# Slot-by-slot messages, an unnormalised router and residual rows behind a square root in a graph-attention and expert layer

## The chip, the cores and the metric

One core of a Trainium2 chip runs the whole kernel in one launch. The metric is device microseconds, from the start of the execution to its end; lower is better.

## The reference, cut to what matters

6250 nodes with 256 features, 106,250 edges sorted by destination (each node has an edge to itself), 8 heads of 32, 8 experts of width 1024, each token to the best two.

```python
e = leaky_relu(a_src[src] + a_dst[dst], 0.2)
e = exp(e - m[dst]);  alpha = e / segment_sum(e, dst)[dst]
out = segment_sum(xh[src] * alpha[:, :, None], dst) + bias
out = (out - mean(out, 0)) * rsqrt(var(out, 0) + eps) * gamma + beta     # over the nodes
x = x + (out + layernorm(x))
logits = layernorm(x) @ Wr + br                                       # 8 experts
top_p, top_idx = top_k(softmax(logits), 2);  weights = top_p / top_p.sum()
x = x + sum over the two of  weights * expert(layernorm(x))               # gelu between two products
```

## The kernel before, in words

Nodes lie in 49 tiles of 128 rows, edges in 879 slots of 128; a slot belongs to one tile of destinations. All five engines run their own streams and meet at semaphores that are written out by hand. There are five stages.

**Stage 1** makes the node table in HBM. **The edge stage** goes over 110 batches of 8 slots (`EB`; the last has 7). GpSimd issues one indirect gather for each slot (line 1072) into a ring of four batches (`gather_ring`); it may go on to batch b when TensorE has summed batch b-4. VectorE runs `score(b)` (four operations of 64 elements, lines 1103 to 1112), its part of preparing the experts' weights (`vector_w1`, `vector_w2`), `sum_picks(b+1)` (line 1095), `message(b)` (line 1117: all 8 slots' rows, 2048 elements, times the heads' weights, which ScalarE's exponential has put into PSUM) and then `adds(b-1)`: for each slot of the batch before, the sum that TensorE made is added to its tile of `acc` (line 1090; the tile's number comes from a register that `load_tiles` fills on VectorE's queue, line 1054). Each addition waits for the one before it. TensorE runs `picks(b+2)` (lines 932 and 1172), `keep_clock` (line 1161: 16 products whose result nobody reads), then one product for each slot (line 1196, two instructions of 264 columns) into four banks (`AGG`), so slot s waits for the addition of slot s-4. When the last slot of a group of 7 tiles is in, `divide` (lines 1127 and 1130) normalises the group; all seven groups become final within the last batches, and before the last batch three of them are divided in one go.

**The norm stage**: TensorE turns `acc` in 13 chunks of 4 tiles (line 1415) through three pairs of banks, VectorE measures each (line 1357), ScalarE puts it back turned (`keep`, line 1428) and, after each chunk, makes two rows of the residual (`scalar_resid`, line 1341). Behind the last chunk stand two more residual rows and then the root of the variance (line 1438). VectorE folds scale and shift from the root, and **stage 3** begins: TensorE makes the normalised rows tile by tile through six banks, VectorE adds the residual (`x1`, line 1481, which waits for its residual row) and measures the row (line 1486), ScalarE copies the router's 8 columns out of the bank (`keep_logits`, line 1719), which frees it, and makes a later residual row.

**Routing** (`vector_route`): a chain of dependent VectorE operations of 392 elements (49 tiles by 8 experts). The logits are scaled and biased, the largest taken off, exponentials made on ScalarE, summed, inverted and multiplied; then the two largest are found and the lists of tokens for each expert built (lines 1644 to 1664, `token_idx`). Meanwhile ScalarE normalises `acc` in 49 rows (`rows`, line 1736) and then issues two transfers of the tokens' weights (`meta`, lines 1752 and 1754). **The expert stage**: GpSimd gathers token rows (line 2013) once `token_idx` and `meta` are in HBM, TensorE turns them (`turn`, line 1932), ScalarE and VectorE split them into two float16 parts, and TensorE computes 56 slots of two products (lines 1951 and 1968).

## Time and profile before

| what | us |
|---|---|
| median of 3 runs (1958.91 to 1962.71) | 1960.81 |
| the profiled execution's own time | 1963.34 |
| its span, from first to last instruction | 1961.5 |
| first gather of the edge stage | 93.9 |
| last addition of the edge stage starts | 1228.00 |
| first tile of stage 3 (line 1481) | 1264.59 |
| first product of the experts (line 1951) | 1368.78 |
| busy: TensorE / VectorE / ScalarE / GpSimd | 1738.8 / 1434.2 / 1118.5 / 1211.7 |

The stages follow each other, so the busy shares over the whole span (89, 73, 57 and 62%) do not say what bounds a stage: TensorE's share contains the products that only keep it busy, and GpSimd's is made in one stage. What a change is worth has to be read where it is made.

### The profile page before, as it was taken

The numbers are of one execution on the slowest core, as the hardware profiler recorded it, in microseconds if no ns is written. First come the engines' busy times: TensorE is split into PE (matmuls) and PEld (weight loads), VectorE is DVE, ScalarE is ACT, GpSimd is POOL, SyncE is SP. The second block draws the span as 40 slices with busy tenths as digits, with TensorE's granted clock in tenths as the row PEclk, the third lists the DMA queues.
The fourth block names the chain that finished last, engine by engine and source line by source line (L and its number), as shares of the span: only waits on it lengthen the run. The fifth ranks groups of instructions, "written<-read, shape, count | busy, mean of one in ns | idle before, by whom it ended". The sixth has DMA issues, their size and how long they took to land.

```text
span 1961.5 us, 36447 instructions
## 1 busy us (share of the span) xinstructions
PE 1738.8 (89%) x10852; PEld 1204.0 (61%) x10852; DVE 1434.2 (73%) x3115; ACT 1118.5 (57%) x2444; POOL 1211.7 (62%) x1150
## 2 busy tenths in 40 slices
PE   7759899899999999999999987645999999999997
PEld 5535554454555555555454544533889898989896
DVE  7787777878778787887777878798666666666664
ACT  5666666767667576676667762661443434343443
POOL 1277777777777777777777774101466565656553
PEclk9979999999999899999999999875999999999999
DMA  5554546455464554555556452387233333333322
GB/s 171 163 147 121 146 141 164 120 154 157 141 165 135 138 157 141 167 143 135 151 140 167 121 138 57 127 297 197 32 49 51 50 50 50 50 51 50 50 42 34
DMA packets 142680, 233.52 MB, mean 119 GB/s; under 512 B 31127, under 2 KB 107553, under 8 KB 141313
## 3 DMA queue, kind: packets, MB, share of 16 engines
q0 software_dynamic: 62800, 147.54, 31.9%
q1 hardware_dynamic: 69765, 81.13, 13.2%
q10 hardware_dynamic: 9932, 2.52, 0.8%
q8 instruction: 101, 1.65, 0.4%
q14 instruction: 82, 0.67, 0.1%
HBM read 188.81 MB, written 43.15 MB: 118 GB/s over the span
## 4 chain that ended last, share of the span: by engine, by line
PE 64%; DVE 15%; issue 8%; DMA 5%; POOL 5%; ACT 2%; DVEq 1%; ACTq 0%; SPq 0%; POOLq 0%
PE bank L1196 15%; PE bank L1951 14%; PE bank L1968 14%; PE bank L1161 12%; POOL gather_ring L1072 5%; PE bank L1172 3%; DVE acc L1090 3%; DMA gather_ring<-node_table,src_slot 2%; DVE gather_ring L1117 2%; PE bank L932 2%; DMA w_stage<-in_L_ffn_W 2%; PE bank L678 1%; PE bank L1932 1%; DVE acc L629 1%; ACT acc L1428 1%
## 5 line engine op out<-in xcount | busy, mean ns | idle before, releaser
L1072 POOL DMA_INDIRECT gather_ring<-node_table,src_slot x879 | 837.5, 953 | 268.2 <-issue 251.7
L1196 PE MATMUL bank<-gather_ring,onehot 128*128 128x264 f32 x1758 | 491.6, 412 | 75.4 <-DVE acc L1090 73.2
L1090 DVE TENSOR_TENSOR acc<-acc,bank 128x264 f32 x879 | 376.9, 429 | 195.1 <-PE bank L1196 123.7
L1196 PEld LDWEIGHTS bank<-gather_ring,onehot 128*128 128x128 f32 x1758 | 303.8, 190 | 252.8 <-DVE acc L1090 208.1
L1161 PE MATMUL bank<-ones 128*128 128x512 bf16 x1760 | 414.3, 390 | 0.0
L2035 POOL DMA_INDIRECT out_rows<-y,token_idx x105 | 202.3, 1926 | 219.8 <-DMA out_rows<-y,token_idx 150.1
L2003 ACT ACTIVATE hid<-bank,cols 128x256 f32<-128x256 f32 (+1 forms) x448 | 210.3, 551 | 141.4 <-PE bank L1951 138.0
L1161 PEld LDWEIGHTS bank<-ones 128*128 128x128 bf16 x1760 | 168.4, 100 | 194.9 <-issue 22.2
L1951 PE MATMUL bank<-xe,w_hi 128*128 128x256 f16 (+1 forms) x1792 | 284.5, 267 | 0.7 <-ACT hid L2003 0.5
L1968 PE MATMUL bank<-w,hid_hi 128*128 x1680 | 278.3, 273 | 0.1
L1217 ACT ACTIVATE onehot<-iota_free,neg_dst 128x128 f32<-128x128 f32 x880 | 267.3, 386 | 0.0
L1117 DVE TENSOR_TENSOR gather_ring<-gather_ring,bank 128x2048 f32<-128x2048 f32 x110 | 250.4, 2276 | 2.0 <-ACT bank L1234 2.0
L2013 POOL DMA_INDIRECT xs<-x_rows,token_idx x105 | 141.9, 1352 | 152.8 <-DVE token_idx L1664 120.8
L1951 PE MATMUL bank<-xe,w_lo 128*128 128x256 f16 (+1 forms) x896 | 236.1, 267 | 0.0
L1234 ACT ACTIVATE bank<-zbuf 128x64 f32<-128x64 f32 x110 | 25.0, 228 | 363.4 <-DVE zbuf L1112 363.4
L1968 PE MATMUL bank<-w,hid_lo 128*128 x840 | 229.0, 273 | 0.0
L1882 DVE TENSOR_SCALAR hid_hi<-hid,cols 128x1024 f16<-128x1024 f32 (+1 forms) x112 | 90.0, 804 | 150.1 <-ACT hid L2003 150.0
L1951 PEld LDWEIGHTS bank<-xe,w_hi 128*128 x1792 | 168.9, 98 | 22.1 <-issue 1.6
L1968 PEld LDWEIGHTS bank<-w,hid_hi 128*128 128x128 f16 x1680 | 164.3, 98 | 20.2 <-issue 0.8
L1989 ACT ACTIVATE xe<-bank 128x512 f16<-128x512 f32 (+1 forms) x56 | 32.0, 571 | 226.4 <-PE bank L1932 226.4
L1172 PE MATMUL bank<-pick_parts,onehotT 128*128 x880 | 114.9, 195 | 44.4 <-DVE gather_ring L1117 15.6
L1172 PEld LDWEIGHTS bank<-pick_parts,onehotT 128*128 128x128 bf16 x880 | 81.6, 98 | 109.4 <-issue 85.8
(288 smaller groups left out, 2049.2 us busy)
## 6 DMA issues: line engine op xcount, KB each, us to landing
w_stage<-in_L_ffn_W SPq DMA_DIRECT2D x16, 1024.0 KB, 7.3
dst_row<-dst_rows SPq DMA_DIRECT2D x110, 128.0 KB, 3.3
gather_ring<-node_table,src_slot POOLq DMA_INDIRECT x879
w_split<-w_out SPq DMA_DIRECT2D x32, 256.0 KB, 2.9
w<-w_split SPq DMA_DIRECT2D x8, 1024.0 KB, 11.9
node_table<-acc SPq DMA_DIRECT2D x24, 264.0 KB
xt<-in_x SPq DMA_DIRECT2D x24, 256.0 KB, 3.0
r_ring<-in_x SPq DMA_DIRECT2D x6, 896.0 KB, 10.6
```

The costliest lines, as they stand in the source:

```text
L1072: e.indirect_dma_start(out=gather_ring[:, b % GB, j, :], out_offset=None, in_=node_table, in_offset=bass.IndirectOffsetOnAxis(ap=src_slot[ ...
L1090: e.tensor_tensor(a, a, bank[AGG[s % len(AGG)]][:, 0:ROW].rearrange("p (a c) -> p a c", a=1), ALU.add).then_inc(added, 1)
L1117: e.tensor_tensor(rows, rows, weights(b).rearrange("p j (h a) -> p j h a", a=1) .broadcast_to([P, EB, HEADS, DH]), ALU.mult).then_inc(mess ...
L1161: e.matmul(idle_bank[:, :].rearrange("p (k n) -> p k n", k=2), halves[:, 0:P], halves.rearrange("p (a n) -> p a n", a=1).broadcast_to([P, ...
L1172: made = e.matmul(bank[PICKS[b % 2]][:, j * 3 * PICK:(j + 1) * 3 * PICK], onehotT[:, b % 2, j * P:(j + 1) * P], pick_parts[:, bass.ds(tile ...
L1196: e.matmul(bank[AGG[s % len(AGG)]][:, 0:ROW], onehot[:, b % OHB, j, :], gather_ring[:, b % GB, j, :], start=True, stop=True).then_inc(summ ...
L1217: made = e.activation(onehot[:, b % OHB, j, :], iota_free[:, :], ACT.Abs, bias=neg_dst[:, s:s + 1])
L1951: made = e.matmul(to, m[:, k, expert, at:at + P].rearrange("p a m -> p (a m)"), xe[:, q, x_, 0:w], start=(k == 0 and n == 0), stop=(k == K ...
L1968: made = e.matmul(bank[YB[q]][:, i * D:(i + 1) * D], a[:, q, c, ts], w2[:, expert, b, c, :].rearrange("p a d -> p (a d)"), start=(c == 0 a ...
L2003: made = e.activation(hid[:, i % HR, c, 0:w], bank[HB[2 * h + c // 2]][:, c % 2 * PW:c % 2 * PW + w], ACT.Gelu, bias=col_of(s, B1_COL + h ...
L2013: e.indirect_dma_start(out=xs[:, t % XR, :], out_offset=None, in_=x_rows, in_offset=bass.IndirectOffsetOnAxis(ap=token_idx[:, t:t + 1], ax ...
L2035: e.indirect_dma_start(out=out, out_offset=bass.IndirectOffsetOnAxis(ap=token_idx[:, t:t + 1], axis=0), in_=y[:, s % 2, t - first_tile(s), ...
```

## The change

In the edge stage the message of a batch is made slot by slot, and behind the message of slot s comes the addition of slot s-3; `sum_picks` and `load_tiles` stand ahead of them, and TensorE waits for each slot's message by itself, runs `picks(b+2)` behind the products of batch b, and spreads its 16 idle products as 8 ahead of the batch and one ahead of each slot. In the norm stage no residual row stands between the chunks: all 24 come behind the root, and a root of a constant is taken ahead of the chunks. In routing the probabilities are never normalised: the two largest of the biased logits are taken, and the weights come from one exponential of their difference (49 elements); two operations on the logits move ahead, between the steps of the last variances, and ScalarE makes two groups of rows before its exponential. At the start of the expert stage `vector_columns` stands behind the first `split_input`, and TensorE's first `turn` ahead of its wait for the experts' numbers.

```diff
-            def message(b):
-                rows = gather_ring[:, b % GB, :, 0:D].rearrange("p j (h d) -> p j h d", d=DH)
-                e.wait_ge(weighed, 2 * b + 1)
-                e.tensor_tensor(rows, rows, weights(b).rearrange("p j (h a) -> p j h a", a=1)
-                                .broadcast_to([P, EB, HEADS, DH]), ALU.mult).then_inc(messages, 1)
+            def message(b, j):
+                row = gather_ring[:, b % GB, j, 0:D].rearrange("p (h d) -> p h d", d=DH)
+                if j == 0:
+                    e.wait_ge(weighed, 2 * b + 1)
+                e.tensor_tensor(row, row, weights(b)[:, j, :].rearrange("p (h a) -> p h a", a=1)
+                                .broadcast_to([P, HEADS, DH]), ALU.mult).then_inc(messages, 1)
+
+            def messages_and_adds(b):
+                for j, s in enumerate(slots_in(b)):
+                    message(b, j)
+                    if s >= ADDS_BEHIND:
+                        add(*divmod(s - ADDS_BEHIND, EB))
...
-            for b in range(LAST_B):
+            for b in range(BATCHES):
+                load_tiles(e, b)
                 score(b)
                 vector_w1(e, b)
                 vector_w2(e, b)
-                sum_picks(b + 1)
-                message(b)
-                if b:
-                    divide_final((b - 1) * EB)
-                    adds(b - 1)
-            adds(LAST_B - 1)
-            score(LAST_B)
-            message(LAST_B)
-            divide_final(LAST_B * EB)
-            adds(LAST_B)
+                if b + 1 < BATCHES:
+                    sum_picks(b + 1)
+                messages_and_adds(b)
+                divide_final(slots_in(b)[-1] + 1 - ADDS_BEHIND)
+            for s in range(USED - ADDS_BEHIND, USED):
+                add(*divmod(s, EB))
             divide_final(USED)
...
             for b in range(BATCHES):
-                if b + 2 < BATCHES:
-                    picks(b + 2)
...
-                keep_clock(e)
+                keep_clock(e, IDLE_PRODUCTS // 2)
                 e.wait_ge(onehot_made, b + 1)
                 e.wait_ge(weighed, 2 * b + 2)
-                e.wait_ge(messages, b + 1)
                 for j, s in enumerate(slots_in(b)):
+                    keep_clock(e, IDLE_PRODUCTS // 2 // EB)
+                    e.wait_ge(messages, s + 1)
...
+                if b + 2 < BATCHES:
+                    picks(b + 2)
...
+            e.activation(sd_col, ones[:, 0:KD], ACT.Sqrt)
             for c in range(CHUNKS):
                 keep(c)
-                for n in range(2 * (c - 2), 2 * (c - 1)):
-                    if 0 <= n:
-                        scalar_resid(e, n)
             e.wait_ge(var_known, 1)
             e.activation(sd_col, var_col, ACT.Sqrt, bias=eps[:, :]).then_inc(sd_made, 1)
-            for n in range(2 * (CHUNKS - 2), RESID_AHEAD):
+            for n in range(RESID_AHEAD):
                 scalar_resid(e, n)
...
             variances(1)
+            pr = prob[:, :, :]
+            e.wait_ge(logits_kept, NT)
+            vector_order.of(e.tensor_tensor(pr, pr, logits[:, :, :], ALU.add))
             second(1)
+            e.wait_ge(vector_order.sem, vector_order.n)
+            vector_order.of(e.tensor_tensor(pr, pr, rs1[:, :].rearrange("p (n a) -> p n a", a=1).broadcast_to([P, NT, NE]),
+                                            ALU.mult))
             gains(1)
...
-            tt(pr, pr, logits[:, :, :], ALU.add)
-            tt(pr, pr, per_tile(rs1[:, :]), ALU.mult)
             tt(pr, pr, per_expert(br_row[:, :]), ALU.add)
-            reduce_e(peak, pr, ALU.max)
-            e.tensor_tensor(pr, pr, per_tile(peak), ALU.subtract).then_inc(logits_shifted, 1)
-            e.wait_ge(exps_made, 1)
-            reduce_e(peak, pr, ALU.add)
-            chain(e, e.reciprocal(peak, peak))
-            tt(pr, pr, per_tile(peak), ALU.mult)
             for c, best in enumerate((w0, w1)):
                 F3 = first[:, c, :, :]
                 reduce_e(best, pr, ALU.max)
+                if c:
+                    e.tensor_tensor(peak, w1, w0, ALU.subtract).then_inc(logits_shifted, 1)
...
-            tt(peak, w0, w1, ALU.add)
-            chain(e, e.reciprocal(peak, peak))
-            vector_order.of(e.tensor_tensor(meta[:, :, 0:1].rearrange("p n a -> p (n a)"), w0, peak, ALU.mult))
-            e.tensor_tensor(meta[:, :, 1:2].rearrange("p n a -> p (n a)"), w1, peak, ALU.mult).then_inc(meta_made, 1)
+            e.wait_ge(exps_made, 1)
+            chain(e, e.tensor_single_scalar(w0, peak, 1.0, ALU.add))
+            chain(e, e.reciprocal(w1, w0))
...
+            for g in range(2):
+                rows(g)
             e.wait_ge(logits_shifted, 1)
-            e.activation(prob[:, :, :], prob[:, :, :], ACT.Exp).then_inc(exps_made, 1)
-            for g in range(GROUPS):
+            e.activation(top[:, 0, :], top[:, 0, :], ACT.Exp).then_inc(exps_made, 1)
+            for g in range(2, GROUPS):
                 rows(g)
...
+            split_input(0)
+            vector_columns(e)
+            e.wait_ge(vector_order.sem, vector_order.n)
             for s in range(2):
                 columns(s)
-            split_input(0)
```

## Rows read from the trace of the kernel before

**Rows 1.** The waits of GpSimd: who waited for whom, us in total, times, longest.
```profile
POOL gather_ring L1072 <- issue: 251.7, 830, 0.3
POOL gather_ring L1072 <- PE bank L1196: 13.4, 48, 0.3
```

**Rows 2.** The gathers by their line: nanoseconds min/median/max, first and last start.
```profile
L1072 POOL DMA_INDIRECT gather_ring<-node_table,src_slot x879: 942/947/2692, 93.9 to 1200.3; - x176
```

**Rows 3.** Timeline of one batch: start us, duration us, instruction, idle before.
```profile
612.19 3.61 PE L1161 MATMUL bank<-ones 128*128 128x512 bf16 x16
...
612.77 0.22 DVE L1103 TENSOR_TENSOR zbuf<-gather_ring,picked 128x64 f32<-128x64 f32 x1
...
614.75 2.28 DVE L1117 TENSOR_TENSOR gather_ring<-gather_ring,bank 128x2048 f32<-128x2048 f32 x1
...
616.94 0.42 DVE L1090 TENSOR_TENSOR acc<-acc,bank 128x264 f32 x1
...
617.58 0.43 DVE L1090 TENSOR_TENSOR acc<-acc,bank 128x264 f32 x1 [0.21 <-DVE acc L1090]
```

**Rows 4.** Timeline of the last batches of the edge stage.
```profile
1148.88 0.94 POOL L1072 DMA_INDIRECT gather_ring<-node_table,src_slot  x1 [0.30 <-issue]
...
1151.73 0.22 DVE L1103 TENSOR_TENSOR zbuf<-gather_ring,picked 128x64 f32<-128x64 f32 x1 [0.97 <-DMA gather_ring<-node_table,src_slot]
...
1200.34 1.81 POOL L1072 DMA_INDIRECT gather_ring<-node_table,src_slot  x1 [0.30 <-issue]
...
1213.25 0.22 DVE L1103 TENSOR_TENSOR zbuf<-gather_ring,picked 128x64 f32<-128x64 f32 x1
...
1228.00 0.43 DVE L1090 TENSOR_TENSOR acc<-acc,bank 128x264 f32 x1 [0.21 <-DVE acc L1090]
```

**Rows 5.** Timeline of the norm stage.
```profile
1230.94 3.68 DVE L1357 BATCH_NORM_STATS2 feat<-bank 128x6 f32<-128x512 f32 x6
...
1232.55 3.05 ACT L1428 ACTIVATE acc<-bank 128x512 f32<-128x512 f32 x6 [17.88 <-DVE feat L1357]
...
1244.18 1.16 ACT L1428 ACTIVATE acc<-bank 128x512 f32<-128x512 f32 x2
...
1244.63 1.29 DVE L1357 BATCH_NORM_STATS2 feat<-bank 128x6 f32<-128x512 f32 x2 [0.66 <-PE bank L1415]
...
1250.31 0.48 DVE L1364 BATCH_NORM_AGGREGATE agg<-feat 128x2 f32<-128x72 f32 x1
...
1255.43 1.28 ACT L1438 ACT_TABLE_LOAD   x1
...
1257.06 0.17 DVE L1385 RECIPROCAL bn_cols<-bn_cols 128x2 f32<-128x2 f32 x1 [3.11 <-ACT bn_cols L1438]
```

**Rows 6.** Timeline, first tile of stage 3.
```profile
1264.59 0.42 DVE L1481 TENSOR_TENSOR acc<-bank,r_ring 128x256 f32<-128x256 f32 x1 [1.89 <-PE bank L1696]
```

**Rows 7.** Timeline of the last variances and the routing.
```profile
1301.36 0.29 DVE L1510 RECIPROCAL rs<-sd 128x21 f32<-128x21 f32 x1 [0.38 <-ACT sd L1728]
...
1304.30 0.57 DVE L1548 TENSOR_TENSOR prob<-prob,br_row 128x392 f32<-128x392 f32 x1
...
1306.53 18.77 ACT L1736 ACTIVATE acc<-acc,shift,gain 128x256 f32<-128x256 f32 x38
...
1308.36 0.56 DVE L1551 TENSOR_REDUCE top<-prob 128x49 f32<-128x392 f32 x1
```

**Rows 8.** Timeline from the tokens' weights to the experts' first products.
```profile
1325.25 27.83 ACTq L1754 DMA_DIRECT2D x_rows<-meta  x1
...
1358.32 1.19 POOL L2013 DMA_INDIRECT xs<-x_rows,token_idx  x1 [120.78 <-DVE token_idx L1664]
...
1367.53 1.09 PE L1932 MATMUL bank<-ident,xs 128*128 128x128 f32 x4 [3.67 <-DMA xs<-x_rows,token_idx]
```

**Rows 9.** Stretches: length, busy us (x instructions) of PE, PEld, DVE, ACT, POOL, clock, DMA share, GB/s.
```profile
1356.30:1358.30 2.00, 0.00 (x0) 0.00 (x0) 1.90 (x5) 0.00 (x0) 0.00 (x0) 0.50 0.00 0
...
1368.70:1371.70 3.00, 2.92 (x14) 2.09 (x15) 0.69 (x1) 0.55 (x1) 1.89 (x2) 0.50 0.32 89
```

More of the change, by code:

```diff
@@ L829, in build_gnn_moe @@
         scalar_order = Order(sem("scalar_order"))
-        AGG = (0, 1, 3, 4)
+        AGG, ADDS_BEHIND = (0, 1, 3, 4), 3
         PICKS = (2, 7)
@@ L1112, in score @@
                 e.tensor_tensor(zbuf[:, 1, :, :], zbuf[:, 1, :, :], zbuf[:, 0, :, :], ALU.subtract).then_inc(scored, 1)
-            def message(b):
-                rows = gather_ring[:, b % GB, :, 0:D].rearrange("p j (h d) -> p j h d", d=DH)
-                e.wait_ge(weighed, 2 * b + 1)
-                e.tensor_tensor(rows, rows, weights(b).rearrange("p j (h a) -> p j h a", a=1)
-                                .broadcast_to([P, EB, HEADS, DH]), ALU.mult).then_inc(messages, 1)
-            def adds(b):
-                load_tiles(e, b)
-                for j in range(len(slots_in(b))):
-                    add(b, j)
+            def message(b, j):
[9 more added lines that the diff above has]
+                        add(*divmod(s - ADDS_BEHIND, EB))
             def divide(g):
@@ L1138, in vector_edges @@
             divided = [0]
-            LAST_B = BATCHES - 1
             e.wait_ge(acc_started, GROUPS)
             sum_picks(0)
-            for b in range(LAST_B):
+            for b in range(BATCHES):
+                load_tiles(e, b)
                 score(b)
@@ L1145, in vector_edges, with keep_clock @@
                 vector_w2(e, b)
-                sum_picks(b + 1)
-                message(b)
-                if b:
-                    divide_final((b - 1) * EB)
-                    adds(b - 1)
-            adds(LAST_B - 1)
-            score(LAST_B)
-            message(LAST_B)
-            divide_final(LAST_B * EB)
-            adds(LAST_B)
+                if b + 1 < BATCHES:
[4 more added lines that the diff above has]
+                add(*divmod(s, EB))
             divide_final(USED)
-        def keep_clock(e):
+        def keep_clock(e, products):
             halves = ones[:, :].bitcast(BF16)
-            for _ in range(IDLE_PRODUCTS):
+            for _ in range(products):
                 e.matmul(idle_bank[:, :].rearrange("p (k n) -> p k n", k=2), halves[:, 0:P],
@@ L1168, in picks @@
                 if b >= 2:
-                    e.wait_ge(messages, b - 1)
+                    e.wait_ge(messages, (b - 1) * EB)
                 tensor_w1_bias(e, b)
@@ L1232, in scalar_edges @@
                 if b >= 2:
-                    e.wait_ge(messages, b - 1)
+                    e.wait_ge(messages, (b - 1) * EB)
                 e.activation(weights(b), zbuf[:, 1, :, :], ACT.Exp).then_inc(weighed, 1)
@@ L1407, in tensor_norm @@
                 if c == 0:
-                    e.wait_ge(messages, BATCHES)
+                    e.wait_ge(messages, USED)
                 if c == 1:
@@ L1578, in vector_route @@
                 if c == 0:
-                    chain(e, e.scalar_tensor_tensor(pr, F3, -2.0, pr, ALU.mult, ALU.add))
+                    chain(e, e.scalar_tensor_tensor(pr, F3, FAR_BELOW, pr, ALU.mult, ALU.add))
             tt(chosen[:, :, :], first[:, 0, :, :], first[:, 1, :, :], ALU.add)
             e.tensor_tensor(chosen[:, :, :], chosen[:, :, :], per_tile(valid[:, :]), ALU.mult).then_inc(chosen_made, 1)
-            tt(peak, w0, w1, ALU.add)
-            chain(e, e.reciprocal(peak, peak))
-            vector_order.of(e.tensor_tensor(meta[:, :, 0:1].rearrange("p n a -> p (n a)"), w0, peak, ALU.mult))
-            e.tensor_tensor(meta[:, :, 1:2].rearrange("p n a -> p (n a)"), w1, peak, ALU.mult).then_inc(meta_made, 1)
+            e.wait_ge(exps_made, 1)
+            chain(e, e.tensor_single_scalar(w0, peak, 1.0, ALU.add))
+            chain(e, e.reciprocal(w1, w0))
+            vector_order.of(e.tensor_copy(meta[:, :, 0:1].rearrange("p n a -> p (n a)"), w1))
+            e.tensor_tensor(meta[:, :, 1:2].rearrange("p n a -> p (n a)"), peak, w1, ALU.mult).then_inc(meta_made, 1)
             def by_expert(psum):
@@ L1683, in vector_route @@
             e.tensor_copy(expert_of_slot[:, :], expert_of_slot_f[:, :]).then_inc(experts_known, 1)
-            vector_columns(e)
         def tensor_stage3(e):
@@ L1738, in rows @@
                 made.then_inc(rows_made, 1)
-            assert GROUPS == RB + 2 and RESID_AHEAD + LATE_AT > RB * NG > 2 * (CHUNKS - 2)
+            assert GROUPS == RB + 2 and RESID_AHEAD + LATE_AT > RB * NG
             for g in range(5):
@@ L1971, in output @@
                 made.then_inc(y_done, 1)
+            for i in range(2):
+                e.wait_ge(rows_stored[i], (STORED[0], ROWS_STORED)[i])
+            turn(0)
             e.wait_ge(experts_known, 1)
-            turn(0)
             for s in range(FS + 1):
```

1 line of the change is left out of this document (removed).

## The prediction

> **What bounds the kernel now.** I read the page's busy shares first, then the chain that ended last, and left both: they mix stages. What decides is read stage by stage in the timeline. In the edge stage the waits of GpSimd come first [rows 1]: 830 of 879 gathers follow the one before after the same 0.3 us, the other 48 were released by TensorE within that same 0.3, so GpSimd was never held up by the ring. With a median gather of 0.947 [rows 2] the pace is 1.25 us a slot, 10.0 a batch, and the whole stretch is 93.9 to 1200.3. VectorE comes second: one batch is 1.98 ahead of the message, 2.19 for it and 8 x 0.64 for the additions, 9.3 in all, since each addition waits 0.21 for its predecessor [rows 3]. So the edge stage can gain only behind the last gather. There VectorE is late: the last batch's score starts at 1213.25 although its gathers were issued at 1200.34, and a batch can be scored 2.85 after its last gather starts (1148.88 to 1151.73, where VectorE did wait for it) [rows 4]. The norm stage is paced by ScalarE: per chunk VectorE measures 1.29 and idles 0.66, and ScalarE spends 1.16 on putting back and the rest on two residual rows; then VectorE waits 3.11 for the root, ahead of which stand two more rows and a table load of 1.28 [rows 5]. Routing is a chain on VectorE alone. From the experts' first product on TensorE sets the time, and nothing there changes.
>
> **Edge loop.** A message of one slot is 256 elements; the addition of 264 takes 0.43, so I take 0.42. Independent VectorE instructions overlap by 0.09 (614.75 + 2.28 against 616.94) [rows 3]. A pair of message and addition is then 0.67, and the 0.21 that an addition waits for its predecessor lies under the message between them; I take 0.70. A batch is 1.98 + 5.6 and some 0.25 for the register load, which no longer lies under a long message: 7.8. That is 1.5 less work than before and 2.2 under the gathers' 10.0, so VectorE waits for gathers instead, and the 106 us that are freed over 110 batches buy nothing. TensorE has the same instructions as before, and with them it never held a gather up [rows 1]. Its reordering costs nothing under the same 10.0. Bounds for the pair: 0.64 below (an addition and its wait) and 0.42 + 0.64 = 1.06 above (nothing overlaps).
>
> **End of the edge stage.** Divisions read and write only `acc`; beside one of them the last gather took 1.81 instead of 0.95 [rows 4]. The new order has one division more among the gathers, which costs the gathers 0.9 (0 to 2.6). Batch 108's last gather, 7 paces before 1200.34, starts at 1191.6; with 0.9 and 2.85 its score starts at 1195.3. Then 1.5 up to the messages, 5.6, and one division. A division: from 1213.25 to 1228.00 before lie 1.3 of score, 2.2 of message, three divisions and 6 x 0.64, so 2.5 each, 2.7 with the wait. VectorE is free at 1205.1; gathers are there at 1204.1 (up to 1206). I take 1205.4. The last batch: 1.3, 7 x 0.70 = 4.9, a division 2.7, and 1.3 up to the start of the last addition: 1215.6 against 1228.00. **Gain 12.4** (10 to 13.5). The two other divisions that stood here now lie ahead, beside waiting time.
>
> **Chunks.** Count from the last addition's start, L. Before, the measuring started at L+2.9 and ended at L+22.3 [rows 5]. After, three chunks still take 3.7 (to L+6.6), but the fourth needs a bank that ScalarE has put back. ScalarE began this at L+4.55, behind its transfers; the new root of a constant puts 1.28 + 0.3 ahead of it, then 1.1 to put back and about 1.2 for TensorE: L+8.2. From there VectorE needs 1.25 a chunk, and TensorE and ScalarE need less: nine chunks and 0.5 for the single tile end at L+20.0; I add 0.5 for transposes at half clock, as the stage starts after an idle TensorE. **Gain 1.8** (0.4 to 3.4).
>
> A table load is 1.28 here, and the reciprocal that waits for the root behind it starts 0.35 after it [rows 5]. The Trainium skill (ScalarE: Activation LUTs, What ACT_TABLE_LOAD costs) adds a drain of about 1.38 us to each switch. No drain shows in these rows; by the page the constant's root would cost the chunks 1.4 more, and the sum would be 1.4 smaller.
>
> **Root.** After: the variance is known 1.8 behind the chunks, ScalarE has the table and no row ahead, so the root is done at 2.2, and VectorE comes to its wait at 3.6 (1250.31 to 1257.06 less 3.11). **Gain 3.1** (2.5 to 3.1).
>
> **Stage 3.** What is late next are the 24 residual rows, at 18.77 / 38 = 0.494 each for rows of this form [rows 7]: 11.9, so from 2.2 to 14.1 behind the chunks, and ScalarE's first copy of router columns, which frees a bank, stands behind them. VectorE starts tile 0 at 3.6 + 7.5 (1257.06 to 1264.59 [rows 5, 6]) = 11.1. Six banks last to tile 6, at 0.66 to 0.7 a tile at 15.1 to 15.3; its product is ready about 1.0 after the first copy, 15.1. ScalarE then catches up (copy and row 0.55 against 0.66). **Cost 0** (to 1.9 if a row takes 0.59).
>
> **Routing.** Between the end of the bias addition (1304.30 + 0.60) and the first maximum (1308.36) stand a maximum, a subtraction, the exponential, a sum, a reciprocal and a product, all gone: 3.46. Two additions and products of 0.60 ahead move to where VectorE waits 0.38 for each root [rows 7]; they spill about 0.15: 1.05. A subtraction of 49 elements comes in: 0.13. The small exponential comes after two groups of rows (14 x 0.494 = 6.9) and a table load, about 0.8 before the choice ends, and what waits for it lies under the count's product on TensorE. **Gain 4.4** (3.8 to 4.6).
>
> **Experts' start.** Gathers need `token_idx` and the landed `meta`. The second meta transfer is issued at 1325.25 and holds its queue 27.8; nothing moves after 1356.3, and the gather starts at 1358.32 [rows 8, 9]. It is issued when the rows are done, and these move only 2.4 ahead of stage 3's end, not 4.4: the cover of 2.0 shrinks to about nothing. Cost 0.3 (0 to 2). Neither moved order gains much: `turn(1)` waits for its rows until 1367.53 [rows 8] in either order, and the first product stands behind it. Gain 0.1. TensorE ran at half clock for the first 3.0 us of the stage [rows 9]; when the clock rises is not tied to the stage, so 1 more or 1.7 less is open both ways.
>
> **Sum.** 12.4 + 1.8 + 3.1 + 0 + 4.4 - 0.3 + 0.1 = 21.5. The span 1961.5 goes to 1940.0 and its execution's 1963.34 to 1941.8; the runs' median, 2.5 below that execution, 1960.81 to 1939.3.
>
> **Rivals.** (a) *Gains eaten by what is late next*: rows at 0.59 stall the six banks by 1.9, meta binds and takes 2.0 of the routing, the last gathers land 2 later, the half clock stays 1 longer. For it: three covers shrink to under 0.5 each. Against: each was worked out as just enough. Gain 14.6 to 17: about 1945. (b) *VectorE becomes the edge stage's bound*: the other side. If the additions keep their own 0.64 and messages 0.42 apart from them (1.06 a pair), a batch is 2.2 + 8.5 = 10.7 against 10.0, 0.7 x 110 = 77 slower less 21: about 2016. It decides from a pair of 1.0 on. For it: `load_tiles` and each addition's register step stand on the same queue. Against: the wait was 0.21 and the message is longer. The Trainium skill (VectorE: DVE Perf Modes, Side-by-side: where the cycles go) gives each instruction some 150 cycles of start, so cutting a message in eight would add about 1.1 us a batch; the rows' overlap takes most of it back, and either way 10.0 is not reached without the lost overlap. (c) *The batch loop also speeds up*, since messages no longer hold VectorE: it would take 1.5 x 110 off, about 1775. Rows 1 exclude it unless the 0.3 hides a wait. (d) *The end isn't shortened*: the last batch is scored late as before, because TensorE's idle products inside the slots delay additions; then only 9.1 remain: 1951.
>
> **How the numbers follow.** Forecast 0.70, (a) 0.18, (b) 0.04, (c) 0.01, (d) 0.07. The forecast's terms have ends 10 + 0.4 + 2.5 - 1.9 + 3.8 - 2 = 12.8 and 13.5 + 3.4 + 3.1 + 4.6 + 0.1 = 24.7, and the clock 1.7; all ends together are unlikely. 1934.5 to 1947 holds the forecast and (a). 0.2% (about 4 us) is what this kernel's measurement can tell from none. Faster 0.95, same 0.01, slower 0.04.
>
> **What would show it.** Message and addition starting about 0.7 apart; gathers still 0.947; GpSimd's first wait at the end of the stage; VectorE waiting for gathers in most batches; the last addition near 1216; no wait of 3 us for the root; tile 6 without a stall; the first maximum right behind the bias addition; the expert gather released by `token_idx` or by a transfer. Gathers above 0.97 us or a pair above 0.95 would make the forecast wrong.

## The result, and the profile after

The changed kernel takes 1942.72 us (median of 4 runs, 1942.01 to 1945.27) against 1960.68 (4 runs, 1958.91 to 1962.71) for the kernel before on the same chip: ratio 0.9908, 95% interval 0.9894 to 0.9922, so 18 us faster. A second set on another chip gave 1946.71 against 1962.67, ratio 0.9918 (0.9904 to 0.9931). The forecast was 1939.3 with a range from 1934.5 to 1947.0.

The profiled execution has a span of 1940.7 (1942.65 with what lies around it), 20.8 under the 1961.5 of before.

**Edge stage.** First the timeline of VectorE inside a batch (line 1118 is a message, line 1090 an addition), then the waits of GpSimd and VectorE for each other's work (us in total, times, longest), with VectorE's waits for gathers in the kernel before at the end:

```profile
610.46 0.41 DVE L1118 TENSOR_TENSOR gather_ring<-gather_ring,bank 128x256 f32<-128x256 f32 x1
610.79 0.42 DVE L1090 TENSOR_TENSOR acc<-acc,bank 128x264 f32 x1
611.13 0.41 DVE L1118 TENSOR_TENSOR gather_ring<-gather_ring,bank 128x256 f32<-128x256 f32 x1
611.46 0.42 DVE L1090 TENSOR_TENSOR acc<-acc,bank 128x264 f32 x1
```

```profile
DVE zbuf L1103 <- DMA gather_ring<-node_table,src_slot: 198.4, 95, 7.3
...
POOL gather_ring L1072 <- issue: 252.8, 837, 0.3
POOL gather_ring L1072 <- PE bank L1193: 12.2, 41, 0.3
```

```profile
DVE zbuf L1103 <- DMA gather_ring<-node_table,src_slot: 25.0, 20, 3.0
```

A message and an addition together take 0.67 from start to start (610.46 to 611.13). GpSimd waits as it did [rows 1], and VectorE now waits 198.4 us for gathers, where it waited 25.0 before.

The end of the stage, where [rows 4] had the last gather at 1200.34, the last score at 1213.25 and the last addition at 1228.00:

```profile
1201.19 0.95 POOL L1072 DMA_INDIRECT gather_ring<-node_table,src_slot  x1 [0.30 <-issue]
...
1202.93 2.02 DVE L1132 TENSOR_TENSOR acc<-acc 128x1792 f32<-128x1792 f32 x1
1204.87 0.22 DVE L1103 TENSOR_TENSOR zbuf<-gather_ring,picked 128x64 f32<-128x64 f32 x1
...
1214.60 0.43 DVE L1090 TENSOR_TENSOR acc<-acc,bank 128x264 f32 x1 [0.21 <-DVE acc L1090]
```

**Norm stage and stage 3.** The rows that answer to [rows 5, 6]: the table load and the root of a constant ahead of the chunks, the aggregate behind the last chunk, the root, the 24 residual rows behind it, the operation of VectorE that needs the root, the first and the third `x1`.

```profile
1218.56 1.28 ACT L1431 ACT_TABLE_LOAD   x1 [12.26 <-issue]
1219.86 0.20 ACT L1431 ACTIVATE bn_cols<-ones 128x2 f32<-128x2 f32 x1
...
1234.57 0.48 DVE L1363 BATCH_NORM_AGGREGATE agg<-feat 128x2 f32<-128x72 f32 x1
...
1236.37 0.29 ACT L1435 ACTIVATE bn_cols<-bn_cols,eps 128x2 f32<-128x2 f32 x1 [1.22 <-DVE bn_cols L1372]
...
1236.57 11.89 ACT L1340 ACTIVATE r_ring<-r_ring,x_shift,rstd 128x256 f32<-128x256 f32 x24
...
1238.11 0.16 DVE L1384 RECIPROCAL bn_cols<-bn_cols 128x2 f32<-128x2 f32 x1
...
1245.28 0.42 DVE L1478 TENSOR_TENSOR acc<-bank,r_ring 128x256 f32<-128x256 f32 x1 [1.54 <-PE bank L1692]
...
1247.54 0.42 DVE L1478 TENSOR_TENSOR acc<-bank,r_ring 128x256 f32<-128x256 f32 x1 [0.37 <-ACT r_ring L1340]
```

The table load now stands ahead of the chunks and the 3.11 wait for the root is gone. The third `x1` did not wait for a residual row, though its line names one: the third of the 24 rows was ready near 1238.1 (1236.57 and three times 0.495). The product that it adds ended at 1247.43, at half clock.

**Routing and the experts' start.** The rows that answer to [rows 7, 8]:

```profile
1284.53 0.56 DVE L1551 TENSOR_TENSOR prob<-prob,br_row 128x392 f32<-128x392 f32 x1
1285.13 0.56 DVE L1554 TENSOR_REDUCE top<-prob 128x49 f32<-128x392 f32 x1
...
1304.04 30.48 ACTq L1752 DMA_DIRECT2D x_rows<-meta  x1
...
1334.22 0.27 DVE L1661 SCALAR_TENSOR_TENSOR token_idx<-upto 128x105 int32<-128x105 f32 x1
...
1339.93 1.19 POOL L2015 DMA_INDIRECT xs<-x_rows,token_idx  x1 [115.79 <-DMA x_rows<-meta]
...
1348.00 0.63 PE L1951 MATMUL bank<-xe,w_hi 128*128 128x256 f16 x2
```

The first maximum follows the bias addition at once. But the first expert gather is no longer released by the token list: the list is ready at 1334.5, the gather starts at 1339.93, released by the transfer of the `meta` columns. Part 4 of the page, the chain that ended last, has the same as one step:

```profile
1304.04 35.00 DMA x_rows<-meta
```

**Where the 20.8 us are**, as differences of the two timelines. Before, the token list's instruction started at 1357.33.

| from, to | before | after | gain |
|---|---|---|---|
| start to first gather | 93.94 | 92.95 | 1.0 |
| first gather to last addition | 1134.06 | 1121.65 | 12.4 |
| last addition to first `x1` | 36.59 | 30.68 | 5.9 |
| first `x1` to last `x1` | 34.36 | 35.10 | -0.7 |
| last `x1` to token list | 58.38 | 53.84 | 4.5 |
| token list to first expert gather | 0.99 | 5.71 | -4.7 |
| expert gather to first expert product | 10.46 | 8.07 | 2.4 |
| first expert product to the end | 592.7 | 592.7 | 0.0 |

### The profile page after: what moved, and what is told of

Its sections match the earlier page's. It is cut to its first block and busy times, and to the rows that moved or that the text cites. A ratio compares the mean times of both kernels' runs of the same rounds, so it can differ in the third digit from the quotient of the medians.

```text
span 1940.7 us, 37977 instructions
## 1 busy us (share of the span) xinstructions
PE 1692.2 (87%) x10851; PEld 1186.6 (61%) x10851; DVE 1420.1 (73%) x3880; ACT 1118.9 (58%) x2445; POOL 1214.0 (63%) x1150
## 3 DMA queue, kind: packets, MB, share of 16 engines
q1 hardware_dynamic: 69765, 81.13, 13.4%
## 5 line engine op out<-in xcount | busy, mean ns | idle before, releaser
L1159 PE MATMUL bank<-ones 128*128 128x512 bf16 x1759 | 553.4, 393 | 76.9 <-ACT gather_ring L1234 65.9
L1193 PE MATMUL bank<-gather_ring,onehot 128*128 128x264 f32 x1758 | 566.7, 405 | 51.0 <-DVE gather_ring L1118 50.6
L1193 PEld LDWEIGHTS bank<-gather_ring,onehot 128*128 128x128 f32 x1758 | 294.8, 195 | 261.4 <-DVE gather_ring L1118 219.3
L1090 DVE TENSOR_TENSOR acc<-acc,bank 128x264 f32 x879 | 367.9, 419 | 18.7 <-PE bank L1193 17.5
L1118 DVE TENSOR_TENSOR gather_ring<-gather_ring,bank 128x256 f32<-128x256 f32 x879 | 359.5, 409 | 0.3 <-ACT bank L1233 0.3
L1103 DVE TENSOR_TENSOR zbuf<-gather_ring,picked 128x64 f32<-128x64 f32 x110 | 24.8, 226 | 202.2 <-DMA gather_ring<-node_table,src_slot 198.4
L1883 DVE SCALAR_TENSOR_TENSOR hid_lo<-hid,cols,hid_hi 128x1024 f16<-128x1024 f32 (+1 forms) x112 | 136.4, 1217 | 4.0
## 6 DMA issues: line engine op xcount, KB each, us to landing
w<-w_split SPq DMA_DIRECT2D x8, 1024.0 KB, 13.8
```

The source lines that it names most:

```text
L1090: e.tensor_tensor(a, a, bank[AGG[s % len(AGG)]][:, 0:ROW].rearrange("p (a c) -> p a c", a=1), ALU.add).then_inc(added, 1)
L1118: e.tensor_tensor(row, row, weights(b)[:, j, :].rearrange("p (h a) -> p h a", a=1) .broadcast_to([P, HEADS, DH]), ALU.mult).then_inc(messa ...
L1159: e.matmul(idle_bank[:, :].rearrange("p (k n) -> p k n", k=2), halves[:, 0:P], halves.rearrange("p (a n) -> p a n", a=1).broadcast_to([P, ...
L1193: e.matmul(bank[AGG[s % len(AGG)]][:, 0:ROW], onehot[:, b % OHB, j, :], gather_ring[:, b % GB, j, :], start=True, stop=True).then_inc(summ ...
L1883: e.scalar_tensor_tensor(hid_lo[:, q, cs, 0:w], hid[:, i % HR, :, 0:w], col_of(s, HS_COL), hid_hi[:, q, cs, 0:w], ALU.mult, ALU.subtract). ...
```

## The experiments

### One part of the change at a time

`x_edges`, `x_norm` and `x_route` are the kernel before with the edge loop, the norm stage, or the routing of the change alone (the last with the order of the first turns).

> The kernel before with the edge loop of the change alone. Theory: the batches' pace stays the gathers', so only the end of the stage moves: last addition 13.4 us earlier, as in the whole change (its trace: 1228.00 to 1214.60), and the time comes out 13 us under the kernel before (near 1947.5). Rival: the edge loop is worth less alone, because the norm stage behind it then still waits for its chunks; under 11 us. If the loop's pace had changed as well, over 30 us.

> The kernel before with the norm stage of the change alone (constant root ahead, residual rows behind the variance's root). Theory: the trace of the whole change has 5.9 us less between the last addition and the first x1, and 0.7 us more between there and the end of the halves' variances, so 5.2 us earlier: near 1955.5. Rival, as predicted: 4.9 with no loss behind it. Rival on the other side: the residual rows, late now, cost stage 3 what the root gave; no change.

> The kernel before with the routing of the change alone, and the order of the first turns with it. Prediction's own step: 4.4 us less (near 1956.3). Theory now: the token list is ready 4.5 us earlier, but the first expert gather then waits for the meta columns, whose last packets land only behind the last four loads of W2; those do not end earlier by as much, so the gather gains under 1 us and the time 0 to 3 us (some 2 us come from the bias load that is then no longer beside the second pair of gathers).

| run | median us | before, same chip | ratio, 95% interval |
|---|---|---|---|
| x_edges | 1951.79 | 1961.91 | 0.9943 (0.993 to 0.9956) |
| x_norm | 1958.29 | 1961.91 | 0.9975 (0.9967 to 0.9984) |
| x_route | 1961.15 | 1961.91 | 0.9997 (0.9988 to 1.0006) |

They save 10.1, 3.6 and 0.8, together 14.5 of the 16 to 18 that the whole change saves. Each is less than its part of the table above. The traces show a loss of the right kind, but the profiled executions of `x_edges` and `x_norm` (1954.95 and 1960.70) lie 3.2 and 2.4 above their medians, so the losses read from them are larger than the medians' share.

*Edges.* From the first gather to the last addition it takes 1121.8, as in the changed kernel, so the gain of this stretch is there (the 13.4 of the expectation held 1.0 of an earlier start). The time fell by less than the 11 of the rival, but not for its reason: from the last addition to the first `x1` it took 35.9, and 36.6 before, so the norm stage did not wait for more. Behind it stage 3 took longer: 38.25 from first to last `x1` in place of 34.36.

*Norm.* Likewise: from the last addition to the first `x1` 31.5 instead of 36.6, then 38.05 for stage 3. Both losses are of one kind: the granted clock of TensorE is half for 6.8 us from tile 30 on, where five `x1` come 1.13 apart instead of 0.66 (2.6 and 2.7 us), and more of the first tiles run at half clock than before (1.2 us in `x_edges`, 0.9 in `x_norm`).

*Routing.* The theory held. The token list is 4.5 earlier against the last `x1` than before; the gather is not (60.5 behind the last `x1`, 59.4 before):

```profile
1350.80 0.27 DVE L1664 SCALAR_TENSOR_TENSOR token_idx<-upto 128x105 int32<-128x105 f32 x1
...
1357.46 1.19 POOL L2018 DMA_INDIRECT xs<-x_rows,token_idx  x1 [122.20 <-DMA x_rows<-meta]
```

By itself the routing part is not to be told from no change.

### What the meta columns wait for

`a_w2_held` is the changed kernel with one wait on SyncE's queue:

```diff
+            e.wait_ge(meta_stored, 16 * 2)
             for ee in range(EARLY_W2, NE):
                 load_w2(ee)
```

> The changed kernel, with the last four loads of W2 held until the meta columns have landed. Theory: the meta columns trickle behind those 4 MB (a few dozen of their packets in 2 us while the loads run), so alone they land near 1320 instead of 1339.0; the first expert gather starts at 1335.2 with the token list, 4.7 us earlier; of this 2 us may go again to the bias load beside the second pair of gathers: 2 to 5 us faster than the changed kernel (1938 to 1941). Rival: the meta columns are slow by themselves, 6,250 packets of 16 bytes; then they land no earlier, the loads end later, and the time is the same or up to 10 us longer.

It took 1942.6 against 1961.91, ratio 0.989 (0.9876 to 0.9905). That is 0.002 to 0.003 better than the changed kernel, with overlapping intervals: the wait is shown by the trace, a gain in time is not.

```profile
1331.18 2.04 SPq L1783 DMA_DIRECT2D w<-w_split  x4
1337.18 0.27 DVE L1661 SCALAR_TENSOR_TENSOR token_idx<-upto 128x105 int32<-128x105 f32 x1
1337.75 1.50 POOL L2016 DMA_INDIRECT xs<-x_rows,token_idx  x1 [113.20 <-DVE token_idx L1661]
...
1341.79 0.35 ACTq L1754 DMA_DIRECT2D b_all<-in_L_ffn_b  x1
```

The gather is released by the token list again, 0.57 behind it. Both theories were half right. In the changed kernel the last tenth of the 6,250 packets of 16 bytes lies between 1321.5 and 1337.7, beside the loads of W2, and ends when these end; without them it ends at 1329.5 with the first packet at 1310.7, so the meta columns also need 19 us of their own beside the rows' stores, and 1320 was wrong. The loads, now late, run beside the gathers, as does the 1 MB bias load: from the token list to the first product are 11.8, against 13.8. So 5.1 are won at the gather and 3.1 of them given back behind it.

The other traces agree. In the eleven profiles where these loads are not held, the last small packet ends 0.5 to 1.0 us behind the last packet of the loads, though the transfer was issued 7.1 to 9.4 us ahead of these four loads. Measured from the last `x1`, it ends at 57.3 in the kernel before and at 57.3 in the changed one, while the token list went from 58.4 to 53.8.

The Trainium skill (DMA: Bandwidth & Descriptors, Queues, rings and completion order) says that each DMA engine takes turns between the queues that have work for it, a packet at a time. The two queues do advance together here; that the small packets all but stop beside the large ones (14 or 15 of them in each 2 us from 1328 to 1336) is what the records show, and the page's turns do not explain by themselves.

`a_meta_early` also sends the large transfer sooner and the bias load later:

```diff
             for g in range(2, GROUPS):
                 rows(g)
-            e.wait_ge(meta_made, 1)
-            e.dma_start(x_rows[0:(NT - 1) * P, D:XROW]..., meta[:, 0:NT - 1, :]).then_inc(meta_stored, 16)
+                if g == 2:
+                    e.wait_ge(meta_made, 1)
+                    e.dma_start(x_rows[0:(NT - 1) * P, D:XROW]..., meta[:, 0:NT - 1, :]).then_inc(meta_stored, 16)
...
                     copy_input(s + 1)
+                if s == 0:
+                    e.wait_ge(experts_known, 1)
+                    e.dma_start(b2_all...).then_inc(b2_loaded, 16)
```

> The changed kernel, with the large transfer of the meta columns issued behind the third group of rows (7 rows of ScalarE behind the Exp) and no longer behind the seventh, the last four loads of W2 held until both meta transfers have landed, and the bias load (1 MB) behind the second turn. Theory: the transfer starts near 1295 and not near 1304, has its 6,250 small packets through by 1320, and the loads of W2 are over before the first gathers of expert rows; the token list then releases the first gather (0.6 us behind it), and the first expert product follows 9 us behind the list, as against 13.8 in the changed kernel and 11.8 with the loads held alone: 4 to 5 us faster. Rival: the small packets only share the same DMA engines with the stores of the rows, so the stores end later by what the meta columns take, and the first gather waits for them: same time.

It took 1939.04, against 1946.71 for the changed kernel beside it on the same chip (0.9876, interval 0.9861 to 0.9892, against 0.9918, interval 0.9904 to 0.9931): 7.7 faster, and the intervals do not meet.

> The changed kernel itself, once more, beside the others on one chip, as their yardstick: 18 us under the kernel before, as in its first runs.

```profile
1328.71 2.11 SPq L1780 DMA_DIRECT2D w<-w_split  x4
1336.11 0.27 DVE L1661 SCALAR_TENSOR_TENSOR token_idx<-upto 128x105 int32<-128x105 f32 x1
1336.68 1.50 POOL L2018 DMA_INDIRECT xs<-x_rows,token_idx  x1 [113.24 <-DVE token_idx L1661]
...
1345.01 0.60 PE L1949 MATMUL bank<-xe,w_hi 128*128 128x256 f16 x2
```

The small packets were through later than expected, at 1327.9, still ahead of the list. From the token list to the first product are now 8.9. In the trace of `after_again` they are 13.3 (1337.02 to 1350.32), so 4.4 are explained here, and the two spans differ by 5.3 (1942.7 to 1937.4). The rest of the 7.7 in the medians is not told apart from the spread between executions. Against `a_w2_held` (11.8 from list to first product) two things changed at once, the earlier transfer with its earlier loads and the later bias load; no run tells how the 2.9 divide between them.

### What holds a gather

`a_div_split` is the changed kernel with the product of a division cut by tile:

```diff
-                e.tensor_tensor(rows, rows, acc[:, tiles(g), D:ROW]..., ALU.mult).then_inc(normalised, 1)
+                for n in range(NG):
+                    made = e.tensor_tensor(rows[:, n:n + 1], rows[:, n:n + 1], acc[:, tiles(g), D:ROW]...[:, n:n + 1]..., ALU.mult)
+                made.then_inc(normalised, 1)
```

> The changed kernel, with each division's product of 128x1792 (2.02 us) given out tile by tile, seven products of some 0.33 us. Theory: a GpSimd gather that meets the long product is held until it ends; four are held by 5.4 us together in the changed kernel, three by 3.5 us in the one before. Short products hold none for longer than 0.4 us, as the messages of 0.41 us show: the last gather starts 4 to 5 us earlier (near 1196.5), the time falls by 4 us; each division is 0.3 us longer, the last one on the path. Rival: what holds a gather is the sum of such products' time, not the length of one; then nothing moves, or 0.3 us is lost.

It took 1941.56, 5.2 under the changed kernel beside it (0.9888, interval 0.9871 to 0.9904, which touches that of the changed kernel, 0.9904 to 0.9931). The timeline around one division, first in the changed kernel, then here:

```profile
1190.53 2.02 DVE L1132 TENSOR_TENSOR acc<-acc 128x1792 f32<-128x1792 f32 x1
1190.72 2.67 POOL L1072 DMA_INDIRECT gather_ring<-node_table,src_slot  x1 [0.30 <-issue]
1193.68 0.95 POOL L1072 DMA_INDIRECT gather_ring<-node_table,src_slot  x1 [0.30 <-issue]
```

```profile
1189.84 2.44 DVE L1133 TENSOR_TENSOR acc<-acc 128x256 f32<-128x256 f32 x7
1190.27 1.15 POOL L1072 DMA_INDIRECT gather_ring<-node_table,src_slot  x1 [0.30 <-issue]
1191.72 1.03 POOL L1072 DMA_INDIRECT gather_ring<-node_table,src_slot  x1 [0.30 <-issue]
```

The gather lasts 1.15 instead of 2.67. Over all divisions, four gathers are held by 5.3 us together in `after_again` and six by 1.0 here, and the last gather starts at 1196.81 instead of 1201.05. Not all of that reaches the end: VectorE reaches the last score 1.3 later behind the last gather (a division's products take 2.44 instead of 2.02), and from the first gather to the last addition it takes 1119.2 instead of 1122.2. So the traces show 3.0 of the 5.2; the spans of the two profiles differ by 3.4.

One part of the expectation's argument was poor: a message takes its weights from a PSUM bank and so does not show what a short product of two SBUF operands does; the run does. What the messages do show is that length alone holds no gather. In the kernel before a message took 2.28, more than a division's product, and the gathers beside them took their usual 0.95:

```profile
614.75 2.28 DVE L1117 TENSOR_TENSOR gather_ring<-gather_ring,bank 128x2048 f32<-128x2048 f32 x1
614.92 0.95 POOL L1072 DMA_INDIRECT gather_ring<-node_table,src_slot  x1 [0.30 <-issue]
616.17 0.95 POOL L1072 DMA_INDIRECT gather_ring<-node_table,src_slot  x1 [0.30 <-issue]
```

Of the 270 gathers that met such a message none took over 0.98. The Trainium skill (VectorE: DVE Perf Modes, Two Vector instructions with no wait between them) says that a VectorE instruction with two SBUF tensors reads the second through an interface that GpSimd shares. That fits: the division's product has two SBUF tensors, and the messages and additions, with one operand in PSUM, hold no gather. No run moves an operand of the same product between SBUF and PSUM, so the operand's place as the cause is argued.

### VectorE's room in a batch

`a_load4` and `a_load8` put idle work behind the messages of the odd slots, or of all:

```diff
                     message(b, j)
+                    if j in (1, 3, 5, 7):       # a_load8: range(EB)
+                        vector_order.of(e.tensor_reduce(spare[:, b % 2, j:j + 1], ones..., AX.XY, ALU.add))
```

> The changed kernel, with four more operations in each batch on VectorE (a sum over 128x256 into a spare column, some 0.35 us each, 1.4 us a batch), behind the messages of the odd slots. Theory: the batches' pace is GpSimd's (10.0 us for 8 gathers, VectorE waits 198 us for them, 1.8 a batch), so the last gather starts where it did (1201.2, to 1 us) and the time moves by less than 3 us. Rival, VectorE close to the bound: 1.4 us a batch appear in full or in part, 30 us or more.

> The changed kernel, with eight more operations in each batch on VectorE (one behind every message; each 128x256 summed into a spare column). With four of them the time did not move. Theory: VectorE's slack in a batch is 1.8 us (198 us of waits for gathers over 109 batches); with eight of them at 0.35 us, 2.8 us, the batch is VectorE's, 10.0 + 1.0 us, and the stage 110 us longer, 2055. Rival: their length lies beside waits that VectorE has anyway inside a batch (for products and exponentials), then less than 30 us.

`a_load4` took 1947.05 in one run (1946.71 for the changed kernel): nothing. `a_load8` took 2034.25. The waits of VectorE for gathers in `a_load4`, and the added operations of `a_load8` by their line:

```profile
DVE zbuf L1104 <- DMA gather_ring<-node_table,src_slot: 56.5, 37, 4.2
```

```profile
L1126 DVE TENSOR_REDUCE spare<-ones 128x1 f32<-128x256 f32 x879 | 360.0, 410 | 0.0
```

Each added operation moves the next one's start by 0.333 (0.41 less the overlap). Four a batch are 439 x 0.333 = 146 us: they came out of the 198.4 us of waits, of which 56.5 are left, and the end did not move. Eight are 879 x 0.333 = 293 us; less 198 that leaves 94, and the last addition came 91.7 later (1306.26). The expectation of 110 had taken 0.35 for an operation. So in this kernel, with the work spread evenly over the batches, the wait of the bottleneck's neighbour is a budget that can be read from the profile to a few per cent.

### The distance of the additions, and the idle products

> The changed kernel, with each addition one slot behind its message instead of three. Theory: an addition then waits for the product of the slot before, which waited for its message: a slot's pair is no longer 0.67 us but the chain of semaphore, product (0.61 us) and addition, near 1.0 us; the batch is 2.6 us longer on VectorE, over its slack of 1.8 us, and the stage longer by up to 0.8 us a batch: 1950 to 2035. Rival: the product of 0.61 us fits behind one pair of 0.67 us; then no change to 1 us.

With `ADDS_BEHIND = 1` the time is 1963.97 in one run, all of the gain gone. In its waits the additions now stand for their products, and the pair takes longer every second slot:

```profile
DVE acc L1090 <- PE bank L1193: 150.9, 434, 3.2
```

```profile
628.68 0.42 DVE L1090 TENSOR_TENSOR acc<-acc,bank 128x264 f32 x1
629.02 0.41 DVE L1118 TENSOR_TENSOR gather_ring<-gather_ring,bank 128x256 f32<-128x256 f32 x1
629.67 0.43 DVE L1090 TENSOR_TENSOR acc<-acc,bank 128x264 f32 x1 [0.24 <-PE bank L1193]
```

Two slots take 1.67 instead of 1.34. The last gather starts 5.6 later (1206.81), and the last addition 28.1 behind it instead of 13.4: 20.3 in all. The same budget accounts for this too: no wait of VectorE for a gather is left. Its waits for products, ahead of the scores and for the picks are 150.9, 36.6 and 26.3 (17.5, 3.7 and 10.1 in the changed kernel), 182 more, and the overlap of 0.09 lost at 434 additions is another 39: 221, or 23 over the 198 that there were.

> The changed kernel, with all sixteen idle products of a batch ahead of its slots and none between them. Theory: the pace of 0.67 us a slot is VectorE's (a message of 0.33 us from start to start, an addition the same), the idle product (0.21 us) between two slot products lies beside it; last addition within 0.5 us of the last gather's distance in the changed kernel (13.4 us), time the same. Rival, as predicted with 0.07: the idle products delay the additions, then the distance gets shorter without them between, or longer because all sixteen stand ahead of the last batch's first slot product (1.9 us more).

It took 1942.37 in one run, and the last addition is 13.43 behind the last gather, as in the changed kernel (13.41). In this run the idle products between slots cost nothing, and neither do sixteen ahead.

### Both improvements together

> The changed kernel with both of what helped it: each division's product given out tile by tile, and the meta columns early, the last four loads of W2 held and the bias load late. Theory: the two act in different stages and add up, 4 to 5 us at the gathers' end and 5 to 7 us at the first expert product: near 1935, a ratio of 0.985 to the kernel before. Rival: the norm stage or the loads of W2 take one of them back; then no better than the better of the two alone (0.9876).

It took 1937.55 against 1962.6, ratio 0.9873 (0.9857 to 0.989), the fastest of all kernels here, 7 to 9 us under the changed kernel by the ratios. But it is not told apart from `a_meta_early` (0.9876). The trace has the first expert product 3.9 earlier than `a_meta_early` (1341.14 to 1345.01) and the end only 2.1 earlier; the experts' stage took 594.1 instead of 592.4. Why it took longer stays open.

## Why the prediction was right, and where it was off, point by point

The mechanism was right in the main: nothing in the batch loop, 12 us behind the last gather, the rest in the stages behind. One term, the meta transfer, was mis-sized by 4.4. The time was forecast 3.4 too low.

- **Edge loop.** Forecast 0.70 a pair and no gain from the loop; measured 0.67, and `a_load4` shows that VectorE's time is worth nothing there. Eight messages at 0.33 are 2.7 a batch where the one message took 2.19, so cutting it cost 0.5, and not the 1.1 that the prediction had from the 150 cycles. The "106 us that are freed" are a slip: 1.5 a batch is 165 over 110 batches, and VectorE's waits for gathers grew by 173.
- **End of the edge stage.** Forecast 12.4, with the last addition at 1215.6; measured 12.4 from the first gather on (1214.60, with a start 1.0 earlier). The last score was forecast for 1205.4 and came at 1204.87. The cost of one division more among the gathers was put at 0.9. It was 1.9: four gathers are held in the changed kernel by 5.3 us together, against three by 3.5 before. That the 12.4 still came out is luck in part, for the last batch was 0.5 shorter than forecast (9.7 from its score to the last addition, not 10.2) and the rest lay in a score put 0.3 later than VectorE was free. Over all profiles the stretch from the first gather to the last addition is 1133.0 to 1134.1 in three with the old loop and 1121.6 to 1122.4 in five with the new one, so 11.6 is the better figure.
- **Chunks and root.** Forecast 1.8 and 3.1; measured 2.3 (the aggregate is 19.97 behind the last addition, 22.31 before) and 3.6 (from there to the first `x1` 10.71, 14.28 before). No drain shows at the table load that was moved: ScalarE's next operation starts at 1219.86, 0.02 behind it. The fourth chunk started 8.55 behind the last addition; the forecast said 8.2, though its own terms add up to 8.4. The 0.5 that it added for half clock did not come.
- **Stage 3.** Forecast 0; measured 0.7 in this trace. No stall at tile 6. The 0.7 is TensorE's clock: three products ran at half clock where two did before. In most of the profiles it costs more (below).
- **Routing.** Forecast 4.4; the token list is 4.5 earlier.
- **Meta transfer: the step that failed.** "Cost 0.3 (0 to 2)" measured 4.7. The step took the transfer as fixed in length, so that it would move with its issue. It is not: it was issued 2.6 us earlier than before against the first loads of W2 (21.9 behind them instead of 24.6), held its queue for 30.5 instead of 27.8, and landed only after the last loads of W2 were through. That was already so before, where its last packet ended at 1356.24 and that of the loads at 1355.40; the prediction saw this end in [rows 9] and took it for the transfer's own. What was late next was the DMA queues' work, and not ScalarE's rows.
- **Experts' start.** Forecast 0.1 for the order of the turns; measured 2.4. The bias load of 1 MB, which before was issued at 1361.85 beside the second pair of gathers (their rows came 4.0 behind the gather's end, here 1.95), was now out before the first gather. This second change of place hid half of the first; it was not in the sum. It is read from the timelines: no run moves the bias load alone.
- **The sum.** The span was forecast at 1940.0 and came at 1940.7. That it came so near is luck in part: against the forecast the start gave 1.0 that nobody had reckoned with, chunks and root 0.5 each, routing 0.1 and the experts' start 2.3, and the meta transfer took 4.4 and stage 3 0.7.
- **From the profiled execution to the median.** The forecast for the median took 2.5 off, since the profiled execution of before lay so much above its median. That of after lies at its median. This conversion is 2.5 of the 3.4 us by which the number is off.

For stage 3, and for executions that take longer than this one, the traces offer a mechanism, argued and not tested. The windows of the stretch behind tile 29, in the changed kernel's first profile and in its second (granted clock is the column behind the five engines):

```profile
1268.00:1272.00 4.00, 4.00 (x37) 3.88 (x36) 3.93 (x14) 2.23 (x12) 0.00 (x0) 1.00 0.32 109
```

```profile
1268.00:1272.00 4.00, 4.00 (x24) 3.81 (x24) 3.10 (x10) 3.25 (x14) 0.00 (x0) 0.64 0.52 176
```

In the second the clock is at its lower level from 1267.4 to 1270.9, after TensorE has stood idle while VectorE took the first half's variances, and in these 4 us it makes 24 products where it made 37. First to last `x1` is 37.0 there and 35.1 in the first; the spans differ by 2.1, about as much. The half clock at tile 30 is 1.2 of this, two more tiles of it at the stage's start 0.7. Nine of the twelve profiles with the new edge loop or norm stage have this stretch, and neither of the two without them (before, `x_route`). The forecast reckoned with a half clock at the chunks and at the experts' start, and not here; at the experts' start it came out even. TensorE's gap ahead of this place is 2.8 to 3.3 us in all fourteen profiles, with the dip and without, so the gap alone does not decide. Whether the change brings this dip or only moves its timing over it, fourteen profiles do not settle.

Of the rivals, (b) did not come, and its point of decision was too high: it was put at a pair of 1.0, but with such pairs `a_load8` was already 92 us longer. By the waits of 198.4 over 879 slots, 0.23 a slot, it lies near 0.67 + 0.23 = 0.9. (d) is out by `a_idle_ahead`. (a) named the meta transfer as one of its parts, with 2.0; that part alone came at 4.7. Of its other parts the gathers' delay came in part (1.0 of 2) and neither the stall of the six banks nor a longer half clock at the experts' start came (2.3 us of it, 3.0 before).

## What to carry to other kernels

When a chain is shortened in front of a join, price the other branch as if it did not move at all: here a transfer of small packets, issued 7 to 9 us ahead of 4 MB of loads on the same DMA engines, ended when these ended. Then order the transfers by who needs them first. The total that an engine waits for the bottleneck was, in the three runs that drew on it here, the work that could be put on it for nothing, to within some 3 us. And behind a bottleneck on GpSimd, look for long VectorE products with two SBUF operands: the same work in pieces of 0.34 us gave 3 us back by the traces and 5 by the medians.

## What the runs showed of the hardware

- A VectorE product of 2.02 us with both operands in SBUF held the gather that met it for up to 1.7 us over its 0.95; seven of 0.34 held two gathers by 0.2 and 0.1. Messages of 2.28 and of 0.41 and additions of 0.42 with one operand in PSUM held none to be seen (median gather 0.947 before and 0.946 after; none of the 270 beside a message of 2.28 over 0.98).
- The meta columns, 98 KB in 6,250 packets of 16 bytes, took 19 us from first to last packet beside the rows' stores in `a_w2_held`, 28 in `a_meta_early`, where more of these stores ran beside them, and 30 in the changed kernel with 4 MB of loads behind. ScalarE's second transfer, of one tile, could be issued at 1304.04 only to hold the queue for 30.48 until the first was nearly through.
- TensorE's granted clock fell to its lower level in the middle of stage 3 in nine of fourteen profiles, at a gap of 2.8 to 3.3 us without a product, and cost 1.1 to 2.7 us by the `x1` there. The same gap stands in the five profiles where it did not fall.
